# Pacing the gathers of a DeepFM and CIN kernel: one event of the units for each gather

## What is computed

```python
emb = embed_table[f_ix, x_idx]                      # [n, 26, 16], gathered rows
lin1 = w1_table[f_ix, x_idx].sum(axis=1, keepdims=True) + w1_bias
s = emb.sum(axis=1)
fm = 0.5 * ((s * s).sum(-1) - (emb * emb).sum(axis=(1, 2)))[:, None]
h = relu(emb.reshape(n, 416) @ mlp_w1 + mlp_b1)
h = relu(h @ mlp_w2 + mlp_b2)
deepfm = lin1 + fm + h @ mlp_w3 + mlp_b3
x0 = emb.transpose(0, 2, 1); last = x0; feats = []
for W in (cin_w0, cin_w1, cin_w2):                  # [128, *, 26]
    last = einsum('ndl,ndf,klf->ndk', last, x0, W); feats.append(last)
cin = concatenate(feats, -1).sum(axis=1) @ lin_w + lin_b
return deepfm + cin
```

## Time and profile before

| what | us |
|---|---|
| time, median of 3 runs | 512.74 |
| lowest and highest run | 511.46, 513.53 |
| span of the profiled execution, first to last instruction | 694.2 |
| POOL busy in it, 360 gathers and little else | 356.6 |
| PE busy in it | 510.3 |
| mean granted TensorE clock in it | 0.863 |

### The profile page before, as it was taken

The page is one execution under the profiler, slowest core; times in us unless marked ns, Lnnn a source line. Parts: engine busy times, 40 slices in busy tenths (PEclk is TensorE's granted clock), DMA queues, the critical chain, the costliest instruction groups (busy, mean ns, idle before and its releaser), DMA issues.

```text
span 694.2 us, 6825 instructions
## 1 busy us (share of the span) xinstructions
PE 510.3 (74%) x2235; PEld 415.1 (60%) x2235; DVE 412.8 (59%) x680; ACT 389.0 (56%) x759; POOL 356.6 (51%) x365
## 2 busy tenths in 40 slices
PE   2897918824696959588695959596886949599988
PEld 2865705723484838476574747475765737478666
DVE  6431227903475748376584847484765848478866
ACT  0321628604464847376574847484665748378875
POOL 6665666774465464637466454547374664510000
PEclk9995666975896979979798989899797979899999
DMA  8836434221111111202111111112021111100000
GB/s 176 163 21 117 88 62 103 7 7 5 5 6 7 4 6 4 7 4 8 5 6 5 5 6 6 6 4 8 3 9 5 6 5 5 6 3 1 0 1 0
DMA packets 21508, 15.57 MB, mean 22 GB/s; under 512 B 12790, under 2 KB 19811, under 8 KB 21347
## 3 DMA queue, kind: packets, MB, share of 16 engines
q0 software_dynamic: 11520, 3.16, 13.5%
q1 hardware_dynamic: 6949, 9.99, 5.9%
q10 hardware_dynamic: 3005, 2.01, 1.4%
HBM read 14.92 MB, written 0.21 MB: 22 GB/s over the span
## 4 chain that ended last, share of the span: by engine, by line
PE 28%; DVE 24%; another core or an unknown queue 18%; ACT 15%; issue 11%; DMA 3%; SPq 0%; DVEq 0%
DVE z_lo L803 5%; ACT ps_s L598 5%; ACT z_hi L591 4%; PE ps_y L1197 4%; PE ps_y L1198 3%; DVE ps_y L946 3%; DVE one_hot L935 3%; PE ps_s L1097 2%; DMA w_space<-cin_w 2%; DVE sums L829 2%; PE ps_q L1111 2%; ACT room_a L597 2%; DVE ps_q L814 2%; DVE emb L950 2%
## 5 line engine op out<-in xcount | busy, mean ns | idle before, releaser
L500 POOL DMA_INDIRECT emb<-rows,idx_raw x360 | 356.3, 990 | 253.7 <-issue 101.4
L803 DVE TENSOR_TENSOR z_lo<-ps_s,z_hi 128x512 fp32r<-128x512 f32 (+1 forms) x192 | 132.1, 688 | 138.9 <-ACT ps_s L598 87.6
L591 ACT ACTIVATE z_hi<-ps_s 128x512 fp32r<-128x512 f32 (+1 forms) x192 | 114.2, 595 | 171.9 <-remote 105.6
L1197 PE MATMUL ps_y<-look_hi,one_hot 128*128 128x442 f32 x224 | 92.6, 413 | 91.4 <-DVE one_hot L935 89.6
L598 ACT ACTIVATE ps_s<-ps_s 128x512 f32<-128x512 f32 (+1 forms) x192 | 113.5, 591 | 0.7
L1111 PE MATMUL ps_q<-z_lo,zw_hi 128*127 128x512 f32 (+1 forms) x192 | 86.9, 453 | 32.6 <-DVE z_lo L803 21.1
L1197 PEld LDWEIGHTS ps_y<-look_hi,one_hot 128*128 128x128 f32 x224 | 49.5, 221 | 101.0 <-DVE emb L950 57.1
L1198 PE MATMUL ps_y<-look_lo,one_hot 128*128 128x442 f32 x224 | 89.3, 400 | 0.0
L946 DVE SCALAR_TENSOR_TENSOR ps_y<-tables,look_place,ps_y 128x442 f32<-128x442 f32 x56 | 37.9, 677 | 78.6 <-remote 70.6
L1097 PE MATMUL ps_s<-xt,pick 128*128 128x512 f32 (+1 forms) x192 | 77.1, 414 | 8.6 <-ACT x L582 5.4
L1113 PE MATMUL ps_q<-z_hi,zw_hi 128*127 128x512 f32 (+1 forms) x192 | 78.9, 411 | 0.0
(11 more groups left out here) (191 smaller groups left out, 765.0 us busy)
## 6 DMA issues: line engine op xcount, KB each, us to landing
emb<-rows,idx_raw POOLq DMA_INDIRECT x360
w_space<-rows SPq DMA_DIRECT2D x2, 728.9 KB
m_space<-rows SPq DMA_DIRECT2D x2, 728.9 KB
w_space<-key_scratch SPq DMA_DIRECT2D x1, 1408.0 KB
w<-cin_w SPq DMA_DIRECT2D x2, 416.0 KB, 4.8
w<-cin_w ACTq DMA_DIRECT2D x2, 416.0 KB, 7.6
w_space<-cin_w SPq DMA_DIRECT2D x2, 416.0 KB
w_space<-cin_w ACTq DMA_DIRECT2D x2, 416.0 KB
```

What stands on the lines that cost most here:

```text
L500: pool.indirect_dma_start(emb[t % EMB][:, f, :], None, rows, bass.IndirectOffsetOnAxis(row_ix[:, t, f:f + 1], 0)).then_inc(gathered[t] if ...
L591: act.activation(z_hi[0:k, c, :], ps[0:k, :], ACT.Square)
L803: z = dve.tensor_tensor(z_lo[0:k, u % NC, :], ps, z_hi[0:k, u % NC, :].bitcast(F32), ALU.subtract)
L1197: pe.matmul(o, one_hot[n % 2][:, j, :], look_hi[i][:, ws], start=(j == 0), stop=False)
```

## The change

The wait of the second gather of each pair goes, and so does the lead of up to three tiles. Instead gathers are numbered n = 0 to 359 through all tiles. From n = 47 on every gather waits for one event, its own: the events are the halves 2 x unit (hi_ready) and 2 x unit + 1 (lo_ready), 28 per tile, and gather n takes half 4 + (n - 47) x 28 // 22, so that 22 gathers follow the 28 halves of one tile. The first is unit 2 of tile 0, and the last unit 200, in tile 14. The waits for a free buffer stay. In the setup the wait for s_blocks moves from gather 34 to 28, gather 34 waits for the first total_ready, and the wait of gather 47 for za_done is replaced by its event of the units; gathers 22 to 33, which went out in one run of twelve, are two runs of six.

```diff
-PER_UNIT = 2
+SETUP_GATHERS = 47
...
-            SETUP_STEPS = {16: (m_done, 1), 22: (b_done, 1), 34: (s_blocks, 1), 41: (by_row_done, 1), 47: (za_done, 1)}
+            SETUP_STEPS = {16: (m_done, 1), 22: (b_done, 1), 28: (s_blocks, 1), 34: (total_ready, 1), 41: (by_row_done, 1)}
+
+            def wait_for_pace(n):
+                if n in SETUP_STEPS:
+                    signal, value = SETUP_STEPS[n]
+                    pool.wait_ge(signal, value)
+                elif n >= SETUP_GATHERS:
+                    half = 2 * NX + (n - SETUP_GATHERS) * 2 * NPROD // (F - LOOKS)
+                    pool.wait_ge(lo_ready if half % 2 else hi_ready, half // 2 + 1)
+
+            n = 0
...
-                    if F * t + f in SETUP_STEPS:
-                        signal, value = SETUP_STEPS[F * t + f]
-                        pool.wait_ge(signal, value)
-                    if t >= EMB - 1 and f and f % PER_UNIT == 0:
-                        behind = s_no(t - EMB, NC + f // PER_UNIT - 1) if t >= EMB else s_no(0, f // PER_UNIT)
-                        pool.wait_ge(hi_ready, behind + 1)
+                    wait_for_pace(n)
...
+                    n += 1
```

## The result

| | median, us | lowest to highest | runs |
|---|---|---|---|
| before | 511.40 | 509.50 to 513.53 | 12 |
| after | 514.25 | 511.88 to 516.48 | 12 |

The ratio after to before is 1.0052, with a 95% interval of 1.0028 to 1.0076: 511.4 x 0.0052 = 2.7 us slower. The forecast was 518, 5.3 us above its base, so the direction came out as forecast and the forecast size was twice what came.

What follows compares the result with a forecast made beforehand. TensorE was taken to bound the timed kernel at 512.7 us. After the change POOL's gather stream would end last: 479.5 to 485.8 plus 2 and 32.8 gives 514.3 to 520.6, middle 517.5, taken as 518; range 504 to 530.

Steps and rivals of the forecast that it cites:

- The long waits belong to the recorded execution: TensorE's late signals, 11 us per tile, are nearly all of the recording and worth nothing to timed runs.
- the fall of the recorded span: Sign in the trace: remote waits shrink or go, so the recorded span falls well below 694.2.
- The rebuilt run: Timed run summed from trace rows: setup 76.0, tile 0 36.0, end 50.3, leaving 26.95 for each of 13 tiles.
- the rival of no change: POOL's 27.5 keeps pace with tiles nearer 27.4, slack of 10.7 covers longer gathers, time stays at 513; chance 0.28.
- The rate: POOL needs 27.5 to 28.0 us for a tile's gathers, so falls 0.5 to 1.7 behind per tile.
- The lead before: Without the change the gather stream's path ends at 500.7 to 507.3, hidden under TensorE's 512.7 by 5 to 12.
- The lead after: Tile 0's events allow no more than gather 65, so the stream's path ends at 514.3 to 520.6.
- The setup at 0: Splitting the setup's run of twelve gathers costs nothing, as nothing waits for the later ones; taken as 0.
- Where it appears: The copy L568 waits for gathers once 10.7 us of slack is used, after 6 to 21 tiles; TensorE's transposes wait behind.
- two more signs: Gathers stand 1.25 or more apart with waits between; the stream's last gather comes little before L556 instead of 50 us ahead.
- The faster rival: TensorE's late signals exist in timed runs, smaller; spaced gathers end them, saving 8.5 us, so 504; chance 0.22.
- C: Theory for the experiments: TensorE's late signals, recorded before the change, are in timed runs too, and the pace acts on them.

Runs made afterwards that it cites:

- e5_again: The kernel before, unchanged, recorded a second time; 511.88 us in one run.
- e3_pace: The changed kernel with s_blocks back at gather 34 and no wait at 28, so the new pace alone; 511.84 us, ratio 0.9996.
- e4_later: The changed kernel with every event eight halves later; 516.43 us, ratio 1.0092.
- e2_setup: The kernel before with only the setup's waits changed and the main loop's pairs left as before; 513.58 us, ratio 1.0042.
- e7_fewer: The changed kernel without the gather of field 0 in tiles 3 to 15 (13 gathers left out); 512.23 us, ratio 1.0004.
- e10_free: The kernel before without the waits of every second gather on a unit; 511.32 us, ratio 0.9998.
- e9_double: The changed kernel with the three later setup waits each moved one step later, for a longer pause at gather 28; 517.11 us, ratio 1.0112.

## Why the prediction was right in direction and wrong in mechanism and size

**The long waits belong to the recorded execution: right.** Before, recorded again, has a span of 510.1 and none of them (e5_again), and none of 11 recordings since shows one. The rule of the Trainium skill that stood beside it ("NOTIFIC — the notification-queue block", section 7.1) would let the writing of records hold an engine up. These runs bear the conclusion out, not the cause: one of twelve recordings had the waits, and what set it apart stays open. That they come with long runs of gathers, as the prediction read them, did not hold: in e5_again the gathers from 22 on go back to back, and there are none. So the fall of the recorded span, forecast as a sign of the change, came without the change as well.

**The rebuilt run: its sum held, its parts did not all.** Tile 0 was put at 36.0 and takes 35.7; the end from tile 14's mark at 50.3 and takes 510.8 - 460.27 = 50.5: both right. The setup was put at 76.0 and ends at 66.1 to 66.7, since the remote wait of 8.35 and more fell away. The tile, as what was left, came out at 26.95 and takes 27.4, and 1.8 lie around the span, not up to 8.5. With that falls the argument against the rival of no change, that 13 tiles at 27.4 would make 518.5: they do take 27.4, and the setup is some 9 us shorter. The measured 2.7 us lie just above the 2.6 that the prediction called the least that can be told.

**The rate: right.** Gathers go at 1.25, 22 of them in 27.5; with the longer ones a tile's gathers take 27.9 in after (334.7 us from the last gather of tile 2 to that of tile 14), against tiles of 27.4. That is 0.5 per tile, the low end of the forecast's 0.5 to 1.7. So a lead, once gone, is not won back. A satisfied wait costs nothing that can be measured: e3_pace, 0.9996.

**"The lead before": failed.** The prediction had gather 47 go out 1.4 before tile 0's mark (74.6 against 76.0) and so had the stream of before hidden "by 5 to 12 us". In e5_again it goes 3.62 after the mark, and the copies of tiles 12 to 14 wait 3.4 us. One error is the subtraction of remote waits from the setup: 4.2 was taken off both, but against e5_again gather 47 had lost 8.5 and the mark 13.4. The other is the path behind the stream. The last gather goes at 471.76, inside the forecast's 465.9 to 472.5, and the last copies, at 476.44, do find their rows; but the prediction's path ran only through these, and the copies that wait stand in the tiles before. Before stands at the edge: there was nothing to use up first.

**"The lead after": failed as a mechanism.** That "no more than gather 65" goes by the end of tile 0 is nearly true, and by chance: gather 66 goes at 101.19, 0.6 before the mark of tile 1, because gather 47 went 6.28 after the mark of tile 0 and the rest followed at their rate. No event held it. The events run ahead of where I had put them: units of tile 0 begin before the mark that I counted from (unit 2 at 61.34, the mark at 66.11), so that each event is there 7 to 14 us before its gather. With eight halves more the first holds show (e4_later).

**The setup at 0: failed, and this is the step that holds the loss.** "Tile 0's 26 all come before that, and tile 1's are copied only late in tile 0, so nothing waits for the later ones". The early copies indeed didn't wait. But POOL's queue has one order: behind gather 28 stand the 331 that follow, and at 1.25 a piece with no pause between them each goes 2.5 later, to the last. The sentence beside it had the price, "some 4 us" if the cover were gone; it was 2.75 in the recording of after, and the cover that I named covers tile 1, not the late tiles. e2_setup shows the loss with this part alone, e3_pace its absence without it, and e7_fewer that it vanishes with the cause still there, once the stream has slack.

**Why 518 and not 514.** The forecast took 13.6 us of lead away (465.9 to 479.5) and set 5 to 12 of cover against it, which left 4.8 in the middle, taken as 518 (5.3). Really 2.5 went, with no cover. Two terms too large, of opposite sign, left a rest twice too large. That the sign came out right is in good part luck: the pauses that were forecast, at the events of tile 0, did not occur, and the one that did was put at 0.

**Where it appears: right.** The copy waits in late tiles, from tile 10's on, and PE behind it, once the slack within a tile is used. But two more signs that I named don't tell the kernels apart: the last gather stands 4.8 ahead of the last copies (472.11 to L562's 476.94) in after and much the same in before recorded again, and gathers do run back to back, with satisfied waits between them, instead of being spaced.

**The faster rival** fell with C. The rule on errata in "VectorE: DVE Perf Modes" of the Trainium skill, that dense increments of semaphores should be spaced, is about a lock. No recording shows one, and e10_free, which drops the old spacing of the gathers altogether, is at 0.9998.

## What to carry to other kernels

A queue that issues back to back, at a rate no faster than its readers use it up, cannot win a pause back: where late readers already wait for it, as in before here, a pause at its start is paid in full, however early it lies (after, e2_setup), and where there is slack behind it the pause is free (e7_fewer). So cost a new wait by all that is queued behind it, and not by its nearest reader alone; a long pause reaches that one too (e9_double). Whether a wait will act at all is read by setting the event's time beside the time at which the instruction would go anyway. And where a recording's span is far from the timed runs, record again before building a sum on differences of it.

## What the hardware showed that I had not expected

The same program recorded twice gave spans of 694.2 and 510.1, with 105.6 us and 70.6 us of remote waits in two lines of the first and none in the second; the medians of its timed runs lay between 511.4 and 512.7 throughout.

Against before, the change with its events 8 halves later cost 4.7 us, of which 2.7 are the change itself; with 12 halves it cost 39.7. In these two recordings a delay is paid once as long as the gathers' events lie ahead of the copies that wait for them, and in every tile where they lie behind.
